# Head of the first sweep of a two-layer graph network: the tables moved behind raw chunk 0, the fourteen node groups put in one row, the raw rows of chunks 1 to 3 normalised a step ahead of their sums

## The reference

```python
h = jnp.maximum(_layernorm(x, axis=-1), 0.0)          # every node row
msgs = h[src]                                         # a row for every edge
neigh = segment_sum(msgs, dst, num_segments=12500)
rst = (1.0 + eps[0]) * h + neigh
x = x + relu(relu(rst @ W1 + b1) @ W2 + b2)
# second layer: t = gelu([relu(layernorm(x))[src], edge] @ Wt + bt), then attention over each
# target's edges, a weighted segment sum of t @ Wv + bv, gelu, and the residual
```

## Time and profile before

| | us |
|---|---|
| median of three runs | 4083.03 |
| span of the profiled execution, its own time here | 6013.6 |
| its first sweep up to the start of POOL's chunk 4 | 154.57 |
| its first sweep up to the start of POOL's chunk 8 | 272.32 |
| POOL idle ahead of chunk 4 | 63.95 |
| TensorE clock granted, mean of the span | 0.633 of full |

### The profile page before, as it was taken

The page is one execution under the profiler, slowest core; times in us unless marked ns, Lnnn a source line. Parts: engine busy times, 40 slices in busy tenths (PEclk is TensorE's granted clock), DMA queues, the critical chain, the costliest instruction groups (busy, mean ns, idle before and its releaser), DMA issues.

```text
span 6013.6 us, 75137 instructions
## 1 busy us (share of the span) xinstructions
PE 3985.3 (66%) x19120; PEld 3071.2 (51%) x19121; DVE 1961.7 (33%) x6898; ACT 1601.6 (27%) x3223; POOL 3043.9 (51%) x3332
## 2 busy tenths in 40 slices
PE   1466666555555555577777777777777777777777
PEld 1344444444434444355555555556555565555655
DVE  4222222222222222233333333333333333333344
ACT  4222222222222222322222222222222222222223
POOL 4566666666666666344444444444444444444442
PEclk5555555555565555577766667766676666766677
DMA  4122222222222222222222222222222222222222
GB/s 128 53 68 66 65 67 66 65 67 67 66 65 68 66 65 67 62 81 77 81 77 77 82 76 80 78 78 81 75 81 77 76 82 76 81 77 77 82 77 65
DMA packets 390065, 446.29 MB, mean 74 GB/s; under 512 B 111768, under 2 KB 314734, under 8 KB 390000
## 3 DMA queue, kind: packets, MB, share of 16 engines
q1 hardware_dynamic: 276940, 233.83, 13.3%
q0 software_dynamic: 100096, 205.20, 13.1%
q10 hardware_dynamic: 12964, 6.53, 0.4%
HBM read 387.05 MB, written 58.21 MB: 74 GB/s over the span
## 4 chain that ended last, share of the span: by engine, by line
another core or an unknown queue 28%; PE 25%; ACT 3%; issue 2%; DVE 0%; DVEq 0%; ACTq 0%
PE attention_sum_ps L1210 10%; PE attention_t_ps L1153 4%; PE attention_pre_ps L1144 3%; PE attention_sc_q L1167 3%; PE attention_row_bank L1189 2%; PE attention_pre_ps L1140 2%; ACT attention_tT L1281 2%; ACT attention_t L1285 1%; PE attention_tot_ps L1219 1%; PE attention_tot_ps L1202 1%; PE attention_sum_ps L1201 0%; DVE attention_lines L1419 0%; ACT acc L1043 0%; PE attention_xm_bank L1175 0%
## 5 line engine op out<-in xcount | busy, mean ns | idle before, releaser
L514 POOL DMA_INDIRECT attention_t<-source_rows,attention_idx x1548 | 1471.4, 951 | 496.0 <-issue 496.0
L514 POOL DMA_INDIRECT gin_hs<-h_rows,gin_idx x1500 | 1455.8, 971 | 486.1 <-issue 486.1
L508 POOL TENSOR_TENSOR spare<-ones 1x1 f32<-1x1 f32 x195 | 36.0, 184 | 1892.9 <-PE attention_sum_ps L1210 1376.9
L1281 ACT ACTIVATE attention_tT<-attention_pre_ps 128x512 f32<-128x512 f32 x391 | 233.5, 597 | 1883.5 <-remote 1381.9
L1167 PE MATMUL attention_sc_q<-attention_qw,attention_tT 128*128 x3128 | 590.7, 329 | 187.7 <-issue 187.6
L1167 PEld LDWEIGHTS attention_sc_q<-attention_qw,attention_tT 128*128 128x128 f32 x3128 | 540.7, 247 | 215.6 <-issue 215.4
L698 PE MATMUL gin_sums<-gin_hot,gin_hs 128*128 128x40 f32 x3136 | 612.2, 383 | 0.0
L1210 PE MATMUL attention_sum_ps<-attention_e_hot,attention_t 128*128 128x96 f32 x3072 | 607.5, 389 | 0.0
L698 PEld LDWEIGHTS gin_sums<-gin_hot,gin_hs 128*128 128x128 f32 x3136 | 598.1, 297 | 18.2 <-issue 12.6
L1210 PEld LDWEIGHTS attention_sum_ps<-attention_e_hot,attention_t 128*128 128x128 f32 x3072 | 591.8, 301 | 21.4 <-issue 20.9
L706 PE MATMUL gin_uy_bank<-acc,gin_w_W 128*128 x196 | 118.6, 708 | 727.2 <-DVE acc L926 727.1
(11 more groups left out here) (215 smaller groups left out, 5319.1 us busy)
## 6 DMA issues: line engine op xcount, KB each, us to landing
attention_evT<-in_edge_attr_cols SPq DMA_DIRECT2D x196, 512.0 KB
attention_t<-source_rows,attention_idx POOLq DMA_INDIRECT x1548
gin_hs<-h_rows,gin_idx POOLq DMA_INDIRECT x1500
attention_qw<-qk_cols SPq DMA_DIRECT2D x98, 160.0 KB, 3.2
attention_cw<-qk_bias_cols SPq DMA_DIRECT2D x98, 132.0 KB, 3.9
attention_fade<-fades SPq DMA_DIRECT2D x98, 132.0 KB, 3.8
gin_x<-in_x SPq DMA_DIRECT2D x98, 128.0 KB
residual_rows<-gin_r SPq DMA_DIRECT2D x98, 128.0 KB
```

Source lines behind the costliest of these rows:

```text
L514: gp.indirect_dma_start(out=out[:, k, :], out_offset=None, in_=rows[:, :], compute_op=op, in_offset=bass.IndirectOffsetOnAxis(ap=idx[:, k: ...
L1281: act.activation(tT[q % 2][:, :], pre_ps[:, :], ACT.Gelu).then_inc(s["tT_sb"], 1)
```

## The change

In the first step DVE and ACT normalise raw chunk 0 first; then DVE makes the tables, then all fourteen node groups follow in a row, and SP issues their fourteen loads in a row, ahead of the load of chunk 0's own rows. The raw rows of chunks 1 to 3 are normalised at the end of the step in which they are `f`, one step ahead of their sums. PE makes the sums of raw chunks where it makes all others, at the end of the step.

```diff
@@ sync
+                        if f and f.at == 0:
+                            for G in range(GROUPS):
+                                node_rows(G)
                         if p0:
                             ...
-                        if f and f.at is not None and f.at < len(groups):
-                            for G in groups[f.at]:
-                                node_rows(G)
@@ tensor
-                        raw = bk and bk.at is not None and bk.at < RAW
-                        if raw:
-                            add_rows(bk)
                         if p2 and not (p1 and p1.last):
                             turn(p2)
                         ...
-                        if bk and not raw:
+                        if bk:
                             add_rows(bk)
@@ scalar
-                        if bk and bk.at is not None and bk.at < RAW:
-                            edge_rows(bk.at)
-                        if f and f.at is not None and f.at < len(groups):
-                            for G in groups[f.at]:
+                        if f and f.at == 0:
+                            edge_rows(0)
+                            for G in range(GROUPS):
                                 node_root(G)
                                 if G > 0:
                                     node_rows(G - 1)
-                            if G == GROUPS - 1:
-                                node_rows(G)
+                            node_rows(G)
                         ...
                             norm2(p1)
+                        if f and f.at is not None and 0 < f.at < RAW:
+                            edge_rows(f.at)
@@ vector
-                next_windows(v, g, w, capped, bank)
...
+                        if f and f.at == 0:
+                            edge_rows(0)
+                            next_windows(v, g, w, capped, bank)
                         if f:
                             wait(v, sums_ready, f.c - 1)
                             onehot_op(v, g, hot[f.j], f.c, g["iota"][:, :]).then_inc(hot_ready, 1)
-                        if bk and bk.at is not None and bk.at < RAW:
-                            edge_rows(bk.at)
-                        ...
+                        if f and f.at == 0:
+                            node_groups()
                         ...
+                        if f and f.at is not None and 0 < f.at < RAW:
+                            edge_rows(f.at)
                         if bk and not bk.last:
                             add_sums(bk)
```

More of the change, by code:

```diff
@@ L67 @@
 AHEAD = 4
-NODE_PARTS = (6, 4, 4)
 MT = 2
@@ L584, in gin_sweeps @@
         one = lambda rows, G: rows[G:G + 1].rearrange("a p t d -> p (a t) d")
-        groups = [range(sum(NODE_PARTS[:n]), sum(NODE_PARTS[:n + 1])) for n in range(len(NODE_PARTS))]
-        assert sum(NODE_PARTS) == GROUPS
         landed = lambda m: 16 * (COLS * (m.g + (1 if m.k else 0)) - (AHEAD if m.k == 1 else 0))
@@ L926, in add_sums, with node_groups @@
                         v.tensor_tensor(nodes, nodes, sums[bk.j][:, 0:SPAN], ALU.add).then_inc(added, 1)
+                    def node_groups():
+                        for G in range(GROUPS):
+                            node_moments(G)
+                            if G > 0:
+                                node_scales(G - 1)
+                        node_scales(G)
                     def step(f, bk, p1, p2, r4, a5):
+                        if f and f.at == 0:
+                            edge_rows(0)
+                            next_windows(v, g, w, capped, bank)
                         if f:
```

## The result

The changed kernel takes 4061.06 us (median of five runs, 4059.63 to 4066.04) against 4083.03 before: ratio 0.9947, 95% interval 0.9936 to 0.9958, so 17 to 26 us faster where 17 was forecast.

What follows compares the result with a forecast made beforehand. POOL issuing gathers nearly all the time was taken as the bound, so an earlier head shortens the run: 16 at chunk 8 (212.0 - 196.0), 17.7 at the gate, 17 taken, 4083 - 17 = 4066 us; range 4051 to 4082.

Steps and rivals of the forecast that it cites:

- The reading: Whole trace: keep durations, drop waits longer than their cause; in a timed run POOL issues gathers nearly all the time.
- The gate: Head, POOL's wait until all fourteen node groups are written: 122.0 before, 104.3 after, 17.7 earlier.
- the 52.8: Head of the kernel before: time from chunk 0's root to the last group's issue, kept from the trace.
- the fetches beside eleven groups: Head: gathers run beside about eleven groups instead of nine; priced between nothing and two groups' delay, taken as nothing.
- The sums behind the gate: Head: sums of chunks 1 to 4 give buffers back; chunk 4's end at 212.0 before, 192.2 after.
- the 1.7 that chunk 5 was to lose: POOL behind the gate: chunk 5's buffer needs chunk 1's sums, so it starts at 126.4 and loses 1.7.
- The term that was mis-sized: Kernel before, chunk 3's sums to chunk 4's: a chain of 12.0, then PE's 16.6, ending at 212.0.
- A: Sums really take 14.3, or groups' delays of 8.8 are real: gain 24 to 34, time near 4054; chance 0.15.
- B: Raw steps take 32 or more instead of 22, POOL's chunk 8 some 10 later than before, slower; chance 0.09.
- C: Raw steps take 26 instead of 22, gain 8, or 27, gain 5: 4078; chance 0.13.
- D: Timed runs issue gathers as slowly as the trace, so POOL can't have stood 31 at the gate: 4083; chance 0.08.
- The signs: Changed trace's head: gate 18 to 25 earlier, chunk 4's sums at least 15 earlier, waits ahead of chunks 7, 8 under 10.

Runs made afterwards that it cites:

- second trace: The kernel before, without an edit, traced again: span 4083.9 us, gate 121.1, POOL's chunk 8 at 214.25.
- stores by SP: Changed kernel with early raw statistics and tables spread between node groups, plus the fourteen node-table stores issued by SP instead of ACT; ratio to before 0.9921.
- row alone: Kernel before with chunk 0, tables and fourteen groups in a row, but raw rows and sums of chunks 1 to 3 still first in their step; ratio 1.0015.
- the halves: On the kernel before: first, only chunk 0, tables and groups in a row, ratio 1.0015; second, only raw rows a step ahead and sums last, 0.9966.
- sums first: Changed kernel with only PE's order undone, raw sums ahead of the products again; ratios to before 0.9999 and, repeated, 0.9997.

## Why the prediction was right, point by point

**The reading.** The trace of 6013.6 us was taken apart into durations, kept, and long waits, dropped. The second trace bears this out: span 4083.9, gathers at (1431.6 + 443.8) / 1500 = 1.25 us where the earlier trace rows had 1.28, and none of the 1377 us of the earlier trace rows.

**The gate.** Forecast 122.0 and 104.3, measured 121.14 and 105.06: 16.1 earlier for 17.7. In before, the 52.8 that the sum kept from chunk 0's root to the last issue are 52.8 in the second trace too (65.21 to 118.05), and the root stands 0.9 earlier than forecast. First raw rows were forecast at 40.6, the first group's at 51.4, the last issue at 101.2; they stand at 41.53, 52.35 and 101.96. That the fetches beside eleven groups cost nothing was right for groups of 3.59; the run with stores by SP shows that there was little room left below it.

**The sums behind the gate.** Ends of chunks 1 to 4 in the change: forecast 126.4, 153.4, 175.6, 192.2; measured 125.3, 152.0, 174.8, 186.5. The last is early because PE made chunk 4's sums in 3.77 instead of 7.05. Two windows show its granted clock (the number ahead of the DMA share) leave the lower level (1.2 GHz, 0.50) after 176, behind a stretch with PE busy for 16.0 of 23 us; what raised it there was not tested:

```profile
153.00:176.00 23.00, 16.04 (x56) 11.94 (x57) 6.78 (x27) 11.96 (x32) 16.04 (x18) 0.50 0.28 70
176.00:196.00 20.00, 15.13 (x72) 10.19 (x71) 8.63 (x38) 7.80 (x22) 15.29 (x17) 0.76 0.34 88
```

Nothing waits for that sum. Chunks 5 to 8 of POOL: forecast 126.4, 153.4, 175.6, 196.0, measured 125.64, 152.18, 174.93, 195.69; the 1.7 that chunk 5 was to lose did not arise. In before the same ends were forecast at 109.3, 151.1, 183.4, 212.0 and stand at 109.1, 150.4, 184.0, 214.1.

**The term that was mis-sized** is the kernel before's part of the sum, by 2.3 us: from chunk 3's sums to chunk 4's I had 28.6, and it took 30.1 (184.0 to 214.1). So chunk 8 differs by 18.6 and not by 16. I then took 17, between 16 at chunk 8 and 17.7 at the gate; in eight of the nine changed kernels the time follows the start of chunk 8 and not the gate, so 16 was the consistent answer of my rows and 18.6 is the measured one. The time agrees with it within the spread: 22 and 19. The forecast of 17 came closer than 16 by mixing in the gate, not by a better reading.

**The rivals.** A fell: neither the 8.8 nor the 14.3 is in the second trace of before or in that of the change. The rule that I named there (the Trainium skill, Perfetto Trace Analysis, "Tensor Engine Instruction (MATMUL, LD_WEIGHTS)": the trace's end of a matmul is computed, not observed) leaves room for longer sums; here the waiting add stands 0.13 to 0.14 behind the computed end (214.20 and 174.93), so the computed end was near the true one. B asked for raw steps of 32 or more: between the starts of the sums of chunks 1 to 4 the change's are 26.7, 22.8 and 15.0, and only kernels that put the sums first come to such steps (32.3 and 33.1 between the sums of chunks 1, 2 and 3 with the row alone). C wanted steps of 26 to 27; the mean of the three is 21.5. D held that POOL can't have stood 31 at the gate of before, and it stood 30.65.

**The signs.** POOL's idle time ahead of chunk 4 (13.5), the first raw rows, the groups, chunk 4's sums (27.6 earlier) and the waits (6.4 ahead of chunk 6, 1.9 ahead of chunk 7, none ahead of chunk 8) came as stated. Two did not. The gate was to come 18 to 25 earlier; it is 49.5 earlier than in the trace with the long waits and 16.1 than in the second trace of before. Chunk 2's sums were to come no later than before; they end at 152.0 for 150.4, and the sum itself had them 2 later. In the working, four groups of 8.8 behind 51.4 end by 86.6 and not by 91, and 60.7, 0.8 and 4.4 make 65.9 and not 66.1; neither carries the forecast.

**What the prediction did not say** is how the halves share the gain. Its prices give +3 and -8 for them (the expectations above), measured were +6 and -14 alone and -18.6 together: the first half pays only behind the second.

## What to carry to other kernels

Where one queue issues nearly all the time, look for the one start behind which both versions run the same code, and price every edit by that start: of nine changed kernels here eight moved in time by what that start moved, within some 3 us, and one (sums first) only within 6, for a reason that stays open. An earlier gate was worth nothing here (row alone) while the work that gives buffers back behind it kept its length; first find which of the two POOL meets last, then move that one. And when a traced execution is half again as long as the timed ones, take its durations, doubt its waits, and trace it again.

## What the runs showed of the hardware that I had not expected

One execution of the same program can be 6013.6 us long under the profiler and another 4083.9: the instructions are the same 75137, a gather of the first sweep takes 971 ns in the first and 954 in the second, and nearly all of the difference is waiting (1377 us for sums of the attention in the first). What made it so was not tried.

The transition between the sweeps takes POOL 28 to 29 us in six of the twelve later traces and 31 to 33 in the other six, for the same kernel too (32.6 and 29.1); by itself this is some 4 us of the 4 to 20 by which timed runs of one kernel differ (the lowest against the highest in each comparison).
